# Attention and routed experts on one core: first loads in another order, filled TensorE waits, and the first normalisation on ScalarE

## The reference

```python
xn = layernorm(x)                              # (x - mean) / sqrt(var + 1e-5)
q, k, v = xn @ Wq.T + bq, ctx @ Wk.T + bk, ctx @ Wv.T + bv      # 16 heads of 16
x = x + tanh(g_xattn) * (softmax(q k^T / 4) v @ Wo.T + bo)
t = layernorm(x)
w, e = top_k(softmax(t @ w_router), 2)         # 8 experts, hidden width 512
moe = sum over the two chosen experts of w * (silu(t @ w1[e]) * (t @ w3[e])) @ w2[e]
shared = (silu(t @ ws1) * (t @ ws3)) @ ws2
out = x + tanh(g_ffn) * (shared / 3 + moe * 2 / 3)
```

## Time and profile before

| what | value |
|---|---|
| median of three runs | 804.16 us |
| the profiled execution: its own time | 805.26 us |
| its span, from the first to the last instruction | 803.4 us |
| mean granted TensorE clock | 0.983 |
| busy: TensorE matmul | 770.1 us (96%) |
| busy: VectorE, ScalarE, GpSimd | 527.6 (66%), 425.8 (53%), 428.1 us (53%) |

### The profile page before, as it was taken

One profiled execution on the slowest core, in us unless ns is written; L12 is line 12 of the kernel. 1 busy time (PEld: TensorE's weight loads), 2 busy tenths in 40 slices (PEclk: granted clock), 3 DMA queues, 4 the chain that ended last, 5 costly groups with the idle time before them and its releaser, 6 DMA issues.

```text
span 803.4 us, 19358 instructions
## 1 busy us (share of the span) xinstructions
PE 770.1 (96%) x6939; PEld 688.8 (86%) x6940; DVE 527.6 (66%) x1108; ACT 425.8 (53%) x717; POOL 428.1 (53%) x498
## 2 busy tenths in 40 slices
PE   4879999999999998899999999999999999999998
PEld 4656777777777776579999999999999999999998
DVE  5757788889888888757665444444444444446897
ACT  5757777777777877662435333333343343343232
POOL 5634446776666654457672666466746584236000
PEclk9879999999999999889999999999999999999999
DMA  6764556776666554243354646444533422228622
GB/s 211 235 213 159 185 186 222 242 240 214 212 218 213 199 185 147 88 164 119 132 141 124 173 143 175 140 131 116 163 87 85 124 53 72 60 60 316 226 91 80
DMA packets 130689, 127.36 MB, mean 159 GB/s; under 512 B 55232, under 2 KB 113088, under 8 KB 130624
## 3 DMA queue, kind: packets, MB, share of 16 engines
q1 hardware_dynamic: 117008, 82.44, 34.8%
q0 software_dynamic: 13616, 44.08, 15.7%
HBM read 75.32 MB, written 50.91 MB: 157 GB/s over the span
## 4 chain that ended last, share of the span: by engine, by line
PE 66%; DMA 9%; POOL 8%; DVE 6%; issue 6%; ACT 2%; SPq 1%; POOLq 1%; ACTq 0%; DVEq 0%
PE bank L585 8%; PE bank L670 7%; PE bank L586 7%; PE bank L587 7%; PE bank_ss L639 5%; PE bank_sm L654 4%; PE bank_sm L585 4%; PE bank_ss L585 4%; PE bank_sm L586 4%; PE bank_sm L587 4%; PE bank_ss L587 4%; DMA y_d<-y_s,y_rows 4%; PE bank_ss L586 4%; POOL w_l L1689 3%; PE bank L677 3%
## 5 line engine op out<-in xcount | busy, mean ns | idle before, releaser
L1302 DVE TENSOR_REDUCE row_max<-bank_sm 128x4 f32<-128x1024 f32 x124 | 151.7, 1223 | 46.0 <-PE bank_sm L654 45.1
L987 ACT ACTIVATE probs_T<-bank_ss 128x1024 f32<-128x1024 f32 x123 | 126.6, 1029 | 21.8 <-PE bank_ss L639 20.4
L1279 DVE TENSOR_TENSOR gT_l<-gg,gT_h 128x1024 fp32r<-128x1024 f32 x49 | 66.8, 1363 | 105.7 <-ACT gT_h L1136 105.7
L585 PE MATMUL bank_ss<-xg_h,w_h 128*128 128x256 f32 x400 | 113.2, 283 | 0.5 <-DVE gg L1488 0.5
L585 PE MATMUL bank_sm<-xg_h,w_h 128*128 128x256 f32 x400 | 113.5, 284 | 0.0
L585 PE MATMUL bank<-w_h,gT_h 128*128 128x256 f32 x392 | 111.2, 284 | 1.8 <-DVE gT_l L1279 1.8
L587 PE MATMUL bank_ss<-xg_l,w_h 128*128 128x256 f32 x400 | 112.9, 282 | 0.0
L586 PE MATMUL bank_sm<-xg_h,w_l 128*128 128x256 f32 x400 | 112.9, 282 | 0.0
L587 PE MATMUL bank_sm<-xg_l,w_h 128*128 128x256 f32 x400 | 112.9, 282 | 0.0
L586 PE MATMUL bank_ss<-xg_h,w_l 128*128 128x256 f32 x400 | 112.9, 282 | 0.0
L586 PE MATMUL bank<-w_h,gT_l 128*128 128x256 f32 x392 | 110.8, 283 | 0.0
(11 more groups left out here) (208 smaller groups left out, 1940.3 us busy)
## 6 DMA issues: line engine op xcount, KB each, us to landing
qk_d<-qk_s SPq DMA_DIRECT2D x64, 256.0 KB, 2.3
w_raw<-wall POOLq DMA_DIRECT2D x27, 512.0 KB
k<-qk_d SPq DMA_DIRECT2D x48, 256.0 KB
q<-qk_d SPq DMA_DIRECT2D x48, 256.0 KB
xq<-xs_d SPq DMA_DIRECT2D x140, 64.0 KB
y_pairs<-y_d POOLq DMA_DIRECT2D x16, 512.0 KB, 9.9
xs_d<-zero_rows SPq DMA_DIRECT2D x8, 514.0 KB
x<-x SPq DMA_DIRECT2D x16, 256.0 KB, 5.1
```

The costliest lines, as they stand in the source:

```text
L585: pe.matmul(out, ah, bh, start=first and k == 0, stop=False)
L987: act.activation(pT[:, 2 * (pv % 4):2 * (pv % 4) + 2, :].rearrange("p h t -> p (h t)"), exp_bank(V.b, pv)[:, :], ACT.Exp, scale=D ** -0.5) ...
L1279: return v.tensor_tensor(dst, ps, high.bitcast(F32), ALU.subtract)
L1302: v.tensor_reduce(mx[B.slot][:, :, :].rearrange("p t (q r) -> p r t q", r=2)[:, :, :, p], max_bank(B.b, p)[:, :].rearrange("p (r t k) -> p ...
```

## The change

- The first normalisation: for batches from 3 on, GpSimd's two passes are gone. VectorE writes the negative mean, GpSimd multiplies it by `rstd` into `shift1` (behind `norm_terms`), and ScalarE does the normalisation in two instructions of 128x256 behind the exponential of step 5 (`norm_ahead`). Batches 0 to 2 are done as before.
- The order of SyncE's first loads and stores (batches 0 to 4) is another one.
- TensorE gets more matmuls that nobody reads: 7 in place of 4 ahead of batch 0's scores, 7 ahead of the turn of batch 1, and twice 8 of 128x256 at the first step of the last iteration (`keep_late`).
- VectorE takes statistics and variance of batch 3 one and two steps later.

```diff
@@ SyncE, first loads @@
             load_x(b2)
             half_out(b0, 1)
             terms_in(b0, 1)
+            half_out(b0, 0)
             load_c(b2)
-            half_out(b0, 0)
+            terms_in(b0, 0)
             load_x(Batch(3))
-            terms_in(b0, 0)
             half_out(b1, 1)
+            half_out(b1, 0)
+            terms_in(b1, 1)
             load_c(Batch(3))
-            terms_in(b1, 1)
-            half_out(b1, 0)
+            terms_in(b1, 0)
+            half_out(b2, 1)
+            first_rows(0)
             load_x(Batch(4))
-            terms_in(b1, 0)
-            first_rows(0)
-            half_out(b2, 1)
             half_out(b2, 0)
             first_rows(1)
@@ TensorE @@
+            def keep_late(n):
+                for k in range(n):
+                    pe.matmul(T2[:, 0:2 * P], counters[:, 0, :], counters[:, :, :].rearrange("p n q -> p (n q)"), start=True, stop=True)
...
                     V, pv = late_pair(C, S, p)
+                    if i == NB - 1 and p == 0:
+                        pe.wait_ge(pos_ok, NB - AHEAD)
+                        keep_late(8)
                     if V:
                         scores_to_exp(V, pv)
+                    if i == NB - 1 and p == 0:
+                        keep_late(8)
                     if B and among_first(B, 1) and p == 0:
-                        keep_warm(SS[:, 0:512], 4)
+                        keep_warm(SS[:, 0:512], 7)
...
+                    if p == 2 and A and A.b == 1:
+                        keep_warm(SS[:, 0:512], 7)
                     if p == 2 and A:
                         pe.wait_ge(xn_ok, A.n(1, 1))
@@ ScalarE @@
+            def norm_ahead(Eb):
+                act.wait_ge(shift1_ok, Eb.n(1, 1 - R))
+                act.wait_ge(xnT_ps, Eb.n())
+                for t in range(TC):
+                    r = act.activation(xn_s[:, t, :], x_s[Eb.x_slot][:, t, :], ACT.Identity, bias=shift1[:, t:t + 1], scale=rstd[:, t:t + 1])
+                r.then_inc(xn_ok, 1)
...
+                    if p == 5 and Eb and not among_first(Eb, R):
+                        norm_ahead(Eb)
                     if p == 6 and A:
                         q_or_k(0, q_bank(A), q_ps, 1)
@@ VectorE @@
             def add_eps(mv, done):
                 settle()
-                if mv is bmv2:
-                    v.tensor_scalar(mean2[:, :], mv[:, :, 0], -1.0, None, ALU.mult)
+                v.tensor_scalar((mean2 if mv is bmv2 else mean1)[:, :], mv[:, :, 0], -1.0, None, ALU.mult)
                 v.tensor_scalar(mv[:, :, 1], mv[:, :, 1], 1e-5, None, ALU.add).then_inc(done, 1)
...
-                    if p == 0 and Eb and Eb.b == R:
-                        stats_ahead()
-                        variance_ahead()
...
                     if p == 1 and Eb and Eb.b != R:
+                        variance_ahead()
+                    if p == 1 and Eb and Eb.b == R:
+                        stats_ahead()
+                    if p == 2 and Eb and Eb.b == R:
                         variance_ahead()
@@ GpSimd @@
-                    moved(po, xnT_ps, Eb.n())
-                    po.tensor_tensor(xn_s[:, :, :], x_s[Eb.x_slot][:, :, :], bmv[:, :, 0:1].to_broadcast([P, TC, E]), ALU.subtract).then_inc(xc_ok, 1)
+                    if among_first(Eb, R):
...
                     if A and among_first(A, 1):
                         leave_low(0, qh_ok, ql_ok)
                     if S2:
                         norm_terms()
                     po.wait_ge(rstd1_ok, Eb.n(1, 1))
-                    po.wait_ge(xc_ok, Eb.n(1, 1))
-                    po.tensor_tensor(xn_s[:, :, :], xn_s[:, :, :], rstd[:, :].unsqueeze(2).to_broadcast([P, TC, E]), ALU.mult).then_inc(xn_ok, 1)
+                    if among_first(Eb, R):
...
+                    else:
+                        po.tensor_tensor(shift1[:, :], mean1[:, :], rstd[:, :], ALU.mult).then_inc(shift1_ok, 1)
```

More of the change, by code:

```diff
@@ L187, in build @@
             rstd = sb(a, "rstd", [P, TC])
+            mean1 = sb(a, "minus_mean1", [P, TC])
+            shift1 = sb(a, "shift1", [P, TC])
             power = sb(a, "power", [P, 1])
@@ L281, in build @@
         x_in = [sem(f"x_in{i}") for i in range(2)]; c_in = sem("c_in")
-        var1_ok = sem("var1_ok"); rstd1_ok = sem("rstd1_ok"); var2_ok = sem("var2_ok"); rstd2_ok = sem("rstd2_ok"); shift2_ok = sem("shift2_ok")
+        var1_ok = sem("var1_ok"); rstd1_ok = sem("rstd1_ok"); shift1_ok = sem("shift1_ok"); var2_ok = sem("var2_ok"); rstd2_ok = sem("rstd2_ok"); shift2_ok = sem("shift2_ok")
         xn_ok = sem("xn_ok"); xc_ok = sem("xc_ok"); xnT_ps = sem("xnT_ps"); xnTh_ok = sem("xnTh_ok"); xnTl_ok = sem("xnTl_ok")
@@ L1765, in one @@
                         context_low()
-                    moved(po, xnT_ps, Eb.n())
-                    po.tensor_tensor(xn_s[:, :, :], x_s[Eb.x_slot][:, :, :], bmv[:, :, 0:1].to_broadcast([P, TC, E]), ALU.subtract).then_inc(xc_ok, 1)
+                    if among_first(Eb, R):
+                        moved(po, xnT_ps, Eb.n())
+                        po.tensor_tensor(xn_s[:, :, :], x_s[Eb.x_slot][:, :, :], bmv[:, :, 0:1].to_broadcast([P, TC, E]), ALU.subtract).then_inc(xc_ok, 1)
                     if A and among_first(A, 1):
@@ L1772, in one @@
                     po.wait_ge(rstd1_ok, Eb.n(1, 1))
-                    po.wait_ge(xc_ok, Eb.n(1, 1))
-                    po.tensor_tensor(xn_s[:, :, :], xn_s[:, :, :], rstd[:, :].unsqueeze(2).to_broadcast([P, TC, E]), ALU.mult).then_inc(xn_ok, 1)
+                    if among_first(Eb, R):
+                        po.wait_ge(xc_ok, Eb.n(1, 1))
+                        po.tensor_tensor(xn_s[:, :, :], xn_s[:, :, :], rstd[:, :].unsqueeze(2).to_broadcast([P, TC, E]), ALU.mult).then_inc(xn_ok, 1)
+                    else:
+                        po.tensor_tensor(shift1[:, :], mean1[:, :], rstd[:, :], ALU.mult).then_inc(shift1_ok, 1)
                 if Eb and not among_first(Eb, R):
```

## The result

The changed kernel takes 809.30 us (median of 13 runs, 804.51 to 812.55), the kernel before 802.35 us (median of 13, 798.36 to 807.13). The ratio is 1.0073, 95% interval [1.0054, 1.0092]: 7 us slower. The forecast was 2.6 us faster, 801.5, with 807.5 as the end of the range.

The account below looks back on a forecast made before the run. TensorE was taken as the bound from 130 to 300 us and from 358 to the end. From 804.16 us, first loads -3.0, normalisation +4.3 and last iteration -3.9 sum to -2.6: 801.5 us, range 794.5 to 807.5.

Parts of the forecast that it names:

- The middle: Iterations with the first normalisation moved to ScalarE: +4.3 us forecast, between 0 and +11.6.
- The bounds by stage: TensorE bounds 130 to 300 us and 358 to the end: savings ahead come out, hold-ups inside are paid in full.
- Part 2: First normalisation on ScalarE: waiting 0.5 us for shift1 delays TensorE 0.43 us in ten iterations, +4.3 us (0 to +11.6).
- Rival (a): The normalisation costs nothing: ScalarE gets shift1 in time or TensorE makes the delay good; 797.3 us, chance 0.25.
- rival (c): VectorE's line 1296 doesn't come earlier, so ScalarE stands 1.16 us more in ten iterations: 808.9 us, chance 0.10.
- the removal of GpSimd's two passes: Two passes of about 1.04 us in each of 13 batches leave GpSimd: 27 us of engine time, counted as 0.
- Part 1: Reordered first loads and early fills: batch 1's scores begin at 38.6 in place of 42.09, -3.0 us (-6 to 0).
- The other end of the range: First loads, -6 us: if the clock holds from 20 to 60 us, some of 8 us at 1.2 GHz halve.
- Part 3: Last iteration: two fills of 8 matmuls keep the clock full from 336 to 346, -3.9 us (-5 to 0).
- If the clock fell elsewhere: A sign that would show the forecast wrong: TensorE's clock falling somewhere other than 336 to 346 us; no size given.
- The base: Starting time of the sum: the 804.16 us median of the runs, 1.1 us below the profiled execution's 805.26 us.

Follow-up runs that it names:

- loads_fills: The changed kernel without its normalisation part, so reordered first loads and added matmuls alone: 800.61 against 801.39 us before, ratio 0.9992.
- after_padded: The changed kernel with long-met waits added on GpSimd, bringing its program back to 662 instructions: 802.25 against 798.50 us before, ratio 1.0044.
- shift_later: The changed kernel with the multiplication for shift1 moved behind context_low on GpSimd, 1.29 us later: 818.58 against 801.39 us before, ratio 1.0226.
- fills_only: The kernel before with only the added matmuls (batches 0 and 1, last iteration): 801.49 against 803.86 us before, ratio 0.9980.
- loads_only: The kernel before with only SyncE's reordered first loads and batch 3's later statistics: 802.77 against 803.86 us before, ratio 0.9978.
- loads_warm: The kernel before with reordered loads and the added matmuls of batches 0 and 1, no late fills: 801.25 against 801.75 us before, ratio 1.0004.
- loads_fills_14: The changed kernel without its normalisation part, with late fills at i = 14 too: 800.26 against 801.39 us before, ratio 0.9987.
- loads_late: The kernel before with reordered loads and late fills at i = 14 and 15, no added warming matmuls: 799.06 against 801.75 us before, ratio 0.9972.
- contexts_sooner: The kernel before with reordered loads, but contexts c(2) and c(3) each ahead of the preceding half out: 798.35 against 798.50 us before, ratio 0.9996.
- norm_mended: The kernel before with normalisation on ScalarE, shift1 ahead of the slices of S2's terms, and padding waits on GpSimd: 801.80 against 801.75 us before, ratio 1.0000.
- norm_only: The kernel before with only the normalisation part of the change: 809.43 against 803.86 us before, ratio 1.0070.
- shift_first: The changed kernel with shift1 computed on GpSimd right behind the root, ahead of the slices of S2's terms: 804.33 against 803.86 us before, ratio 0.9999.
- fill_14_too: The changed kernel with small fill matmuls in the idle places of i = 14 too: 807.26 against 798.50 us before, ratio 1.0095.

## Why the prediction was wrong

- **How far off, and where.** Forecast -2.6, measured +7.0: 9.6 us. Parts 1 and 3 were to give 6.9 us and gave 0.8 (`loads_fills`, ratio [0.9969, 1.0015]): 6.1 us of the miss are terms that were mis-sized. The middle was to cost 4.3 us and cost 7.5 (the changed kernel over `loads_fills` in the same set): 3.2 us more, and there a step of the working failed, not a size (the sets differ, so the two don't add to 9.6).
- **The bounds by stage were right.** What holds TensorE in the middle is paid in full: 1.26 us a beat for 1.29 us.
- **Part 2, its mechanism, was right, and its size a little high.** ScalarE waits 0.42 us for `shift1` (forecast 0.5), line 1295 took 0.17 us (it is line 1317 there), the beat is 0.30 us longer (forecast 0.43), from the copy of q of i = 1 to that of i = 12 that makes 2.8 us (219.3 in `after_padded`, 216.5 in `loads_fills`; forecast 4.3). Rival (a), a middle for free, was the kernel in which `shift1` goes first; rival (c) was not this one, but `shift_later` shows what a longer wait costs: 1.71 us of wait, 17 us in all. That its 808.9 us lie beside the measured 809.3 is chance: ScalarE waited 0.42 us at that place, not over 1.
- **The step that failed is the removal of GpSimd's two passes: "That is 27 us of an engine that waits for ScalarE anyway, so it is worth 0."** It was costed by the engine's time alone. Two instructions fewer in each iteration move all later ones to other places in its program, and the first scatter to one where, by the landing of its packet, its code is still on the way: 2.5 to 4.8 us of stall in the profiled executions, with the clock's fall behind it up to 6.2 us, and over runs 3 us between the changed kernel and `after_padded`. Neither the sum nor a rival had it, and no row of the trace of before shows a stall there (its first scatter waited 0.19 us). With it the sum of the middle is 4.4 us in one profiled execution and 8.6 in the other (225.6 between the copies of q against 217.0).
- **Part 1, -3.0, was mis-sized: -1.1 over runs, with an interval from -3.5 to 0.** The terms went as early as forecast (32.80 for 33.7), and the first row maximum behind x(4)'s statistics ran at 43.4 as forecast, but the scores stopped at 40.4, not 38.6, behind VectorE's row maximum, for which I had no term. The other end of the range was misread too: the earlier trace rows have TensorE at half clock for 17 of the 40 us from 20 to 60, not 8. In the changed kernel's profiled execution it was 7 us, and the copy of q of i = 1 came 0.4 us earlier.
- **Part 3, -3.9, was right for i = 15 and incomplete.** The clock is full from 336 to 346. The two fills took 1.14 us each, for 0.94 forecast and holes of 1.04. The changed kernel's fills at i = 15, the turn of the row maximum behind them, and its first matmul of the experts:

```profile
339.96 1.21 PE L634 MATMUL bank<-counters 128*128 128x256 f32 x8
341.10 0.51 PE L646 MATMUL bank_ss<-q,k 64*128 64x256 f32 x4
341.54 1.21 PE L634 MATMUL bank<-counters 128*128 128x256 f32 x8
342.68 0.38 PE L715 MATMUL bank<-consts,row_max 128*16 128x128 f32 x2
...
361.56 0.38 PE L587 MATMUL bank_sm<-xg_h,w_h 128*128 128x256 f32 x1
```

18.9 us from the turn (342.68) to the experts, where before it was 22.9 (334.84 to 357.75): 4.0 us, as forecast. "If the clock fell elsewhere" came true: at i = 14, where holes of 1.07 and 0.46 us stand unfilled, before and after, 3.8 us were lost in the profiled execution (i = 15 starts 7.8 us later than before, 4.1 of which were lost by i = 12). I had read the holes of the last iteration only. Over runs the fills are worth less than 4 us: 2.4 in `fills_only` (an interval from -3.5 to +0.2), nothing between `loads_only` and `loads_fills` (1.1 and 0.8 below before), and the late fills alone 0.6 (`loads_warm` to `loads_fills_14`) and 1.6 (`loads_only` to `loads_late`), across sets. Without them the clock doesn't fall in each execution either: in `contexts_sooner` it didn't.
- **The base.** The sum started from three runs and one profile; 13 runs put before at 802.35, 1.8 us lower than the three.

## What to carry to other kernels

When work is moved between engines, look for the smallest instruction that the moved work waits for and what stands ahead of it on its queue: here one of 0.20 us, put one place earlier, was worth 0.3 us in each iteration of the trace, and over runs nearly all that the change had lost. When instructions leave or enter an engine's straight-line program, look at every long "issue" gap that is new, and at whether an instruction packet lands behind the last instruction ahead of it; a few idle instructions move the cut, and in `norm_mended` they cost nothing that could be measured. An idle hole behind which the clock falls is to be looked for at every place of the same form, not at the last one alone, and a term that depends on the clock wants many runs, not one profile of each kernel.

## What was not expected of the hardware

- With its first scatter as the 69th instruction GpSimd stood 2.46 to 4.76 us ahead of it in five profiled executions out of five, until 1.4 to 1.9 us behind the landing of a packet of 8 KB of its code; with the scatter as the 74th or 79th it was 0.18 or 0.19 us in every one of 13, though in eight of them the packet came under queues as full. That the wait is for this packet is an inference from these times and from the padding.
- Behind this stall, in the middle of a dense stretch, TensorE's granted clock fell to 0.50 in four of the five executions (`norm_only`, `shift_first`, `fill_14_too`, the changed kernel's second), but not in the changed kernel's first.
- The same program had the clock at 0.50 over the whole of 322 to 332 us in one execution, and at 1.00 from 312 to 352 in another (the changed kernel, twice).
